# A two-layer attention and expert kernel: the zeros behind the experts' rows written a batch earlier, the gate columns folded into the linear product

## The reference, cut to what matters

```
# layer 0
o   = paged_attention(x)             # 8 heads, window 256, K/V rows through block tables
t   = o @ Wo.T
lg  = clip(t @ gate_w.T, -50, 50)    # 8 experts
top_w, top_i = top_k(lg, 2);  rw = softmax(top_w)
x   = x + t @ W.T + contrib(t, rw, top_i)     # a sparse part M[e] per expert, from 4096 masked cells
# layer 1
h   = x @ W1.T + lora(x, adapter of the batch) * scaling
p   = softmax(h @ gate1);  s, i = top_k(p, 2);  s = s / sum(s)
x   = x + sum over the two chosen experts of s * alpha * (gelu(h @ fc1[e] + b1[e]) @ fc2[e] + b2[e])
```

## Time and profile before

| | |
|---|---|
| median of 3 runs | 1142.62 us (1139.97 to 1144.23) |
| the profiled execution | 1142.49 us, span 1140.7 us |
| mean granted clock of TensorE | 0.929 of full speed |
| busy: TensorE, VectorE, ScalarE, GpSimd | 88%, 47%, 36%, 27% |
| HBM traffic over the span | 147 GB/s |
| zeros to `rows_d` | 2 x 8 DMAs of 258 KB, 3.7 us to landing |

### The profile page before, as it was taken

One profiled execution on the slowest core, in us unless ns is written; L12 is line 12 of the kernel. 1 busy time (PEld: TensorE's weight loads), 2 busy tenths in 40 slices (PEclk: granted clock), 3 DMA queues, 4 the chain that ended last, 5 costly groups with the idle time before them and its releaser, 6 DMA issues.

```text
span 1140.7 us, 18892 instructions
## 1 busy us (share of the span) xinstructions
PE 999.9 (88%) x5042; PEld 678.0 (59%) x5043; DVE 535.7 (47%) x2106; ACT 405.5 (36%) x1185; POOL 306.6 (27%) x250
## 2 busy tenths in 40 slices
PE   5999949899999899808889997999289999999994
PEld 2464447677777677604444445666167777777772
DVE  5768874455455677442334442555423333333331
ACT  3434313555565555301111111112124444444440
POOL 3000140357654141111334440233202221122221
PEclk9989956899999999958999998999689999999998
DMA  8756540354453343238787745884443333333330
GB/s 266 238 215 214 198 162 21 94 131 112 127 157 114 112 153 112 75 130 228 210 221 125 137 84 166 303 332 160 149 139 67 68 62 72 72 65 67 57 59 2
DMA packets 82417, 156.25 MB, mean 137 GB/s; under 512 B 16023, under 2 KB 28999, under 8 KB 80768
## 3 DMA queue, kind: packets, MB, share of 16 engines
q1 hardware_dynamic: 40336, 86.99, 23.2%
q0 software_dynamic: 25520, 45.11, 19.1%
q10 hardware_dynamic: 16512, 23.60, 6.5%
HBM read 94.05 MB, written 73.19 MB: 147 GB/s over the span
## 4 chain that ended last, share of the span: by engine, by line
PE 64%; DVE 14%; issue 8%; DMA 7%; DVEq 2%; ACT 2%; SPq 2%; POOL 0%; ACTq 0%; POOLq 0%
PE ps L630 44%; PE ps L711 7%; PE ps L636 4%; DMA acc<-R,tok_i 4%; PE ps L701 3%; PE ps L694 3%; DVE R L1334 1%; DVE R L1326 1%; DVE R L1344 1%; PE ps L875 1%; DMA R<-rows 1%; DVE R L1337 1%; ACT R L977 1%; SPq L392 1%; SPq L391 1%
## 5 line engine op out<-in xcount | busy, mean ns | idle before, releaser
L630 PE MATMUL ps<-R 128*128 128x128 f32 (+4 forms) x2640 | 676.4, 413 | 20.1 <-DMA R<-in_x_t 11.5
L630 PEld LDWEIGHTS ps<-R 128*128 128x128 f32 x2640 | 395.9, 194 | 259.3 <-issue 242.4
L636 PE MATMUL ps<-ident,R 128*128 128x128 f32 x504 | 77.8, 286 | 67.2 <-DMA R<-rows 54.4
L602 POOL DMA_INDIRECT out_x<-R,tok_i x39 | 60.9, 1562 | 252.2 <-DVEq L1773 165.1
L530 POOL DMA_INDIRECT rows<-R,slot_i x64 | 67.1, 1048 | 203.5 <-DVEq L1521 180.6
L636 PEld LDWEIGHTS ps<-ident,R 128*128 128x128 f32 x504 | 62.2, 152 | 94.9 <-issue 77.1
L711 PEld LDWEIGHTS ps<-R 128*128 128x128 f32 x768 | 96.4, 199 | 20.0 <-ACT R L993 16.6
L711 PE MATMUL ps<-R 128*128 128x64 f32 x768 | 99.4, 281 | 4.8 <-ACT R L993 4.8
L1410 DVE CUSTOM_DVE_ANT_0 R<-ps,R 128x384 f32<-128x384 f32 x128 | 66.0, 553 | 75.2 <-issue 75.0
L987 ACT ACTIVATE R<-R,nmx 128x384 f32<-128x384 f32 x128 | 77.5, 607 | 58.8 <-DVE nmx L1410 58.7
L602 POOL DMA_INDIRECT acc<-R,tok_i x39 | 60.6, 1553 | 128.4 <-DVE R L1675 123.3
(11 more groups left out here) (281 smaller groups left out, 924.8 us busy)
## 6 DMA issues: line engine op xcount, KB each, us to landing
R<-rows SPq DMA_DIRECT2D x78, 258.0 KB, 3.4
R<-in_fc ACTq DMA_DIRECT2D x16, 1024.0 KB, 5.6
m_buf<-R SPq DMA_DIRECT2D x8, 1024.0 KB, 5.1
R<-m_buf SPq DMA_DIRECT2D x16, 512.0 KB, 3.9
R<-acc SPq DMA_DIRECT2D x32, 256.0 KB, 5.4
rows<-zrow SPq DMA_DIRECT2D x16, 258.0 KB, 3.7
new_kv<-R SPq DMA_DIRECT2D x16, 256.0 KB, 2.1
qn<-R SPq DMA_DIRECT2D x16, 256.0 KB, 2.5
```

Source lines behind the costliest of these rows:

```text
L602: po.indirect_dma_start(out=sums[s], out_offset=bass.IndirectOffsetOnAxis(ap=tok_i[:, s:s + 1], axis=0), in_=y_sb[s], in_offset=None, boun ...
L630: m = pe.matmul(out, lhs(k), rhs(k), start=(k == 0 and first), stop=(k == KC - 1 and last))
L636: m = pe.transpose(out[:, k * P:(k + 1) * P], src[:, k * P:(k + 1) * P], ident[:])
```

## The change

Zeros: `end_i` is taken before the last batch is placed, so the zeros cover three times 128 rows from there; SyncE issues them then and waits for nothing, and GpSimd waits for them before it sends the last batch's rows. Cells: 9, 9 and 10 in GpSimd's batches 1 to 3; pieces of `m_buf` are fetched from period 3 on, and one addition step is made in each step from 8B + j = 34 on. The periods are all written out. The last tile's projection of attention goes to banks 2 and 3, upper half first, and ScalarE copies it. `choose` makes one instruction of two. Linear stage: `w1_t` and `lora_b` have 520 columns, each product is made in halves of 256 and 264, ScalarE copies both halves and the logits, and the softmax over eight is replaced by one exponential of the difference of the two chosen logits. Allocations and semaphore names are left out below.

```
@@ periods @@
-            period(0, "first", 0, 0)
-            with eng.Fori(0, 2) as i:
-                period(2 * i + 1, "mid", 1, i)
-                period(2 * i + 2, "mid", 0, i)
...
+            for B in range(NB):
+                period(B, "first" if B == 0 else "last" if B == NB - 1 else "mid", B % 2, (B - 1) // 2)
@@ SyncE @@
             for b in range(NB - 1):
+                for m in range(4 * b - 14, 4 * b - 12) if b >= 4 else ():
+                    sp.wait_ge(S["m_done"], m - 1)
+                    fetch_m(m)
                 sp.wait_ge(S["bk"], uses(b, "mid" if b else "first")["q0"] + 1)
...
-                if b == 4:
+                if b == 3:
                     sp.wait_ge(S["mscat"], 16 * ST)
                     for m in range(2):
                         fetch_m(m)
-                if b >= 5:
-                    for m in range(7 * (b - 5) + 2, min(7 * (b - 4) + 2, 16)):
-                        sp.wait_ge(S["m_done"], m - 1)
-                        fetch_m(m)
+                for m in range(4 * b - 12, 4 * b - 10) if b >= 4 else ():
+                    sp.wait_ge(S["m_done"], m - 1)
+                    fetch_m(m)
+            for m in range(14, 16):
+                sp.wait_ge(S["m_done"], m - 1)
+                fetch_m(m)
@@ zero_ends @@
-                    end = sp.value_load(end_i[0:1, e:e + 1], min_val=0, max_val=ROWS - P * NE)
-                    sp.dma_start(rows_d[bass.ds(end, P), :].rearrange("p (h n) -> p h n", h=2),
-                                 zrow[:].unsqueeze(1).broadcast_to([P, 2, DX // 2])).then_inc(S["zrows"], 16)
-                sp.wait_ge(S["zrows"], 16 * NE * n)
+                    end = sp.value_load(end_i[0:1, e:e + 1], min_val=0, max_val=NE * REGION - 3 * P)
+                    sp.dma_start(rows_d[bass.ds(end, 3 * P), :].rearrange("(p a) (h n) -> p (a h) n", a=3, h=2),
+                                 zrow[:].unsqueeze(1).broadcast_to([P, 6, DX // 2])).then_inc(S["zrows"], 16)
@@ GpSimd @@
-                t = 4 + 7 * (b - 1)
-                add = b <= 4
+                t = 4 + 9 * (b - 1)
+                add = b <= 3
...
                 if add:
-                    cells(t + 6)
+                    for u in range(t + 6, t + 9 if b < 3 else ST):
+                        cells(u)
             for b in (NB - 2, NB - 1):
                 po.wait_ge(S["r_slot"], b + 1)
+                if b == NB - 1:
+                    po.wait_ge(S["zrows"], 16 * NE)
                 for t in (2 * b, 2 * b + 1):
+                    if t == NT - 1:
+                        po.wait_ge(S["e_row"], 2)
...
                 po.wait_ge(S["r_slot"], NB + b + 1)
+                if b == NB - 1:
+                    po.wait_ge(S["zrows"], 16 * NE * 2)
@@ TensorE, behind attention and linear @@
-            project(at, "a1")
-            project(at, "h1")
+            pe.wait_ge(bc, at["o1"] + 1)
+            half("h1", 2).then_inc(S["e_in"], 1)
+            half("a1", 3).then_inc(S["e_in"], 1)
...
-                    chunks(ps[:, 4 + s, :], lambda k: x1_t[s][:, k, :], lambda k: w1_t[:, k, :], last=False)
+                    chunks(ps[:, 4 + s, 0:D // 2], lambda k: x1_t[s][:, k, :], lambda k: w1_t[:, k, 0:D // 2], last=False)
...
-                    pe.matmul(ps[:, 4 + s, :], xa_t[s], lora_b[:], start=False, stop=True).then_inc(S2["c_h"][s], 1)
-                    wait(pe, S2["c_lg"][s], i)
-                    chunks(ps[:, 6 + s, 0:NE], lambda k: x1_t[s][:, k, :], lambda k: w1_g[:, k, :], last=False)
-                    pe.matmul(ps[:, 6 + s, 0:NE], xa_t[s], b_g[:], start=False, stop=True).then_inc(S2["c_g"][s], 1)
+                    pe.matmul(ps[:, 4 + s, 0:D // 2], xa_t[s], lora_b[:, 0:D // 2], start=False, stop=True).then_inc(S2["c_h"][s], 1)
+                    chunks(ps[:, 6 + s, 0:DG - D // 2], lambda k: x1_t[s][:, k, :], lambda k: w1_t[:, k, D // 2:DG], last=False)
+                    pe.matmul(ps[:, 6 + s, 0:DG - D // 2], xa_t[s], lora_b[:, D // 2:DG], start=False, stop=True
+                              ).then_inc(S2["c_g"][s], 1)
@@ ScalarE, linear @@
-                ac.activation(x2_rows[:, 2 * i + s, 0:D], ps[:, 4 + s, :], ACT.Copy).then_inc(S2["c_x2"][s], 1)
+                ac.activation(x2_rows[:, 2 * i + s, 0:D // 2], ps[:, 4 + s, 0:D // 2], ACT.Copy)
+                ac.wait_ge(S2["c_g"][s], i + 1)
+                ac.activation(x2_rows[:, 2 * i + s, D // 2:D], ps[:, 6 + s, 0:D // 2], ACT.Copy)
+                if s == 0:
+                    ac.wait_ge(S["r_sel"], NB + i)
+                ac.activation(lg[:, s, :], ps[:, 6 + s, D // 2:DG - D // 2], ACT.Copy).then_inc(S2["c_x2"][s], 1)
@@ VectorE @@
-                    TT(t1[:], src[:], b3(best2[:, c, :]), ALU.is_equal)
-                    ve.drain()
-                    TT(t1[:], t1[:], rb(rev[:]), ALU.mult)
+                    for t in range(2):
+                        ve.scalar_tensor_tensor(t1[:, t, :], src[:, t, :], best2[:, c, t:t + 1], rev[:], ALU.is_equal, ALU.mult)
...
                     if j == 7 and last:
+                        ends()
                         row_low(at, "a2", 2 * B)
-                    if isinstance(B, int) and 8 * B + j >= 42:
-                        for _ in range(ADDS[j]):
-                            next(adds, None)
+                    if 8 * B + j >= 34:
+                        next(adds)
...
                 if not first:
-                    for _ in choose(1):
+                    routed(i - 1)
+                    for _ in place1(i - 1):
                         pass
...
+                    if not more:
+                        ends()
```

More of the change, by code:

```diff
@@ L281, in program @@
                 "last": ("a0", "h0", "o1", "a1", "h1", "o0", "rt", "a2"),
-                "after": ("h2", "o1", "a1", "h1", "rt")}
+                "after": ("h2", "o1", "rt")}
         NF, NM, NL = (len(USES[k]) for k in ("first", "mid", "last"))
@@ L719, in tail, with half @@
                 turn4(ps[:, 0, :], o_sb).then_inc(bk, 1)
+            def half(x, b):
+                lo, hi = (0, D // 2) if x[0] == "a" else (D // 2, DG)
+                return chunks(ps[:, b, 0:hi - lo], lambda k: o_t[:, k, :], lambda k: w_o[:, k, lo:hi])
             def project(at, x):
                 wait(pe, bc, at[x])
-                if x[0] == "a":
-                    chunks(ps[:, 0, 0:D // 2], lambda k: o_t[:, k, :], lambda k: w_o[:, k, 0:D // 2]).then_inc(bk, 1)
-                else:
-                    chunks(ps[:, 0, 0:DG - D // 2], lambda k: o_t[:, k, :], lambda k: w_o[:, k, D // 2:DG]).then_inc(bk, 1)
+                half(x, 0).then_inc(bk, 1)
             def cell_sums(at):
@@ L848, in _ @@
             pe.wait_ge(S["w5"], 48)
+            pe.wait_ge(S["w1_ok"], 1)
             def turn_x1(i, s):
@@ L1090, in outs @@
                         turned(i + 1, s)
+                    if s == 0 and (not isinstance(i, int) or i > 0):
+                        soft(i - 1)
                 ac.drain()
@@ L1466, in choose @@
                     ve.drain()
-                    TT(t1[:], src[:], b3(best2[:, c, :]), ALU.is_equal)
-                    ve.drain()
-                    TT(t1[:], t1[:], rb(rev[:]), ALU.mult)
+                    if c == 1:
+                        gap = TT(diff[:], best2[:, 1, :], best2[:, 0, :], ALU.subtract)
+                        if layer == 1:
+                            gap.then_inc(S["r_l"], 1)
+                    for t in range(2):
+                        ve.scalar_tensor_tensor(t1[:, t, :], src[:, t, :], best2[:, c, t:t + 1], rev[:], ALU.is_equal, ALU.mult)
                     ve.drain()
@@ L1507, in place @@
                 TT(run[:], run[:], t2[:, 0, :], ALU.add)
+                if layer == 1:
+                    TS(rs2[:], ew[:, 0, :], 1.0, None, ALU.add)
                 ve.drain()
                 TT(run[:], run[:], t2[:, 1, :], ALU.add)
+                if layer == 1:
+                    ve.reciprocal(best2[:, 0, :], rs2[:])
                 yield
+                ve.drain()
                 TT(t3, chosen_e[:], t1[:].unsqueeze(1).broadcast_to([P, 2, 2, NE]), ALU.mult)
+                if layer == 1:
+                    TT(best2[:, 1, :], best2[:, 0, :], ew[:, 0, :], ALU.mult)
                 ve.drain()
@@ L1527, in place0, with ends @@
                 return place(a_rows, t, 0, ps[:, 0, 0:2 * NE], ps[:, 0, 2 * NE:4 * NE], (bc, 1))
+            def ends():
+                ve.drain()
+                CP(end_i[:], run[:])
+                ve.drain().then_inc(S["r_end"], 1)
             def tiles():
@@ L1534, in tiles @@
                 ve.drain()
-                CP(end_i[:], run[:])
-                ve.drain().then_inc(S["r_end"], 1)
                 step(TT(ntf[0][:], run[:], region0[:], ALU.subtract))
@@ L1699, in place1, with routed @@
                 ve.memset(junk[:, 3:4], 0.0)
+                ve.wait_ge(S["r_lexp"], i + 1)
+                ve.memset(junk[:, 2:3], 0.0)
```

(32 more changed lines are left out.)

45 lines of the change are left out of this document (17 added, 28 removed).

## The result

The changed kernel took 1147.87 us (median of 20 runs, 1144.01 to 1153.65), the kernel before on the same chip 1143.08 us (median of 20, 1139.97 to 1146.10). The ratio is 1.0041, with a 95% interval of 1.0029 to 1.0053: slower, by less than the half per cent that I had set as the bound. The forecast was 1129.7 with 1112 to 1142, so the median lies above the range; the prediction gave a result within half a per cent of no change a chance of 0.12, and a gain beyond it 0.78. The profiled execution took 1146.05 us, with a span of 1143.1 us (before: a span of 1140.7).

The account below looks back on a forecast made before the run. TensorE's matrix products were taken as the bound (64% of the last-ending chain), plus a few stalls. From 1142.49 us: linear -10.0, gap 1 -11.6, gap 2 +7.8, attention +1.0, together -12.8, giving 1129.7 us; range 1112 to 1142.

Parts of the forecast that it names:

- Z: Time from the zeros' first issue to their landing, before each expert stage; forecast 24 us for 6.34 MB at 334 GB/s.
- From the landing to TensorE: First gap, from zeros landed through the last four blocks and the row fetch to TensorE's first turn: 10.6 us.
- The zeros' bound by transfer and not by issues: Both gaps: transfer outlasts seven issue distances of 1.34 us; the rival, bound by issues, said 1112.3 us, chance 0.12.
- The first sign named for being wrong: Both gaps: the forecast would be wrong if the zeros landed in under 16 or over 30 us.
- a burst three times the old one's time: Rival for both gaps: zeros take 38 us, total +15.2 us, 1157.7 us; chance 0.08.
- Gap 1: Between attention and layer 0's experts: zeros issued a batch early start TensorE at 505.9 instead of 517.48 us, -11.6.
- Gap 2: Between linear stage and layer 1's experts: the larger zeros, covered by one short round, delay TensorE by 7.8 us.
- E: End of TensorE's last gate product in the linear stage; zeros were forecast to start 0.4 us behind it.
- Attention: Period 5's stall goes (-6.8 us), but late corrections and a late addition add waits; net +1.0, ends -6.8 and +7.2.
- its two waits: Attention: TensorE waits 2 to 5 us for corrections, addition 5.8 us late; overlapping, some 7.8 us with the slow clock.
- Linear stage: Gate columns folded into wider products save 1.5 us a round, 12.0 over eight; less 2 for late sums, -10.0 us.
- The limit of 375 GB/s: Linear stage: most that DMA could move, against 391 GB/s needed in a 12.15 us round, so fc2 loads may slip.

Follow-up runs that it names:

- Kernels 1: Zero bursts alone, without the computation: 1032-byte packets as in the changed kernel moved 234 GB/s, the 6.34 MB taking 27 us; whole run 247.07 us.
- kernel 4: Changed kernel with zeros over 256 instead of 384 rows per expert (4.23 MB): 1128.98 us, ratio 0.9880 to the kernel before.
- kernel 5: Changed kernel with the same 384 rows of zeros sent in half as many packets of 2064 bytes: 1134.60 us, ratio 0.9822 to the kernel before.
- kernel 9: Bursts alone, without the computation, varying packet size and start: 337 to 343 GB/s at multiples of 1024 or 1280 bytes, 238 and 205 otherwise.
- Kernel 3: Changed kernel with GpSimd's fetches of keys and values ahead of batch 3's cells and blocks: 1150.17 us, ratio 1.0090 to the kernel before.
- Kernel 7: Changed kernel with old 128-row zeros, cells 8, 8, 8, 4, additions from turn 38, m_buf fetches moved up: 1121.83 us, ratio 0.9717 to the kernel before.
- kernel 2: Changed kernel with the zeros alone undone (128 rows per expert, after the last batch): 1124.99 us, ratio 0.9854 to the kernel before.
- kernels 6: Changed kernel with zeros and the order of cells, additions and fetches undone: 1129.74 us, ratio 0.9773 to the kernel before.
- kernel 8: Kernel 7 with zeros in whole rows, four DMAs issued by SyncE and four by ScalarE: 1113.20 us, ratio 0.9633 to the kernel before.

## Why the prediction was wrong

**The failing step is the burst's duration.** The prediction said: "In 14 us the queue moved 2.64 MB at a 56.5% share: 334 GB/s when busy", and so Z = 24 us. Measured were 32.4 and 31.7. As it counts in both gaps, it is 8.4 + 7.7 = 16.1 us, and the whole miss in spans is 2.4 + 12.8 = 15.2. Kernels 1, 4, 5 and 9 show the cause: 1032-byte packets without gaps run at about 238 GB/s once a burst lasts, and at 333 only in its first 2 us. By kernel 9 it is where they start: all fast packets of this size started on multiples of 1024 or 1280 bytes, and of those 1032 bytes apart nearly all start elsewhere. In the whole kernel only the size of the packets was changed (kernel 5), not their place. The old burst came in eight short pieces 1.34 us apart, as the rates of the kernel before from 500 to 514 us show, in slices of 0.35 us:

```profile
GB/s 0 94 211 293 246 234 340 355 221 203 339 348 121 62 357 319 21 159 354 242 0 233 354 168 0 310 348 97 50 351 330 24 139 351 266 0 0 0 0 0
```

Most pieces reach 348 to 357 and are over before a slow stretch could begin. So the rate was read rightly and applied to a stretch in which it doesn't hold. That the whole miss is so near the burst's alone is in part luck: attention came 3.8 us worse than forecast and the linear stage 4.7 us better.

**What held in that part.** From the landing to TensorE: 10.8 against 10.6. The zeros' bound by transfer and not by issues: yes (an issue every 2.5 us instead of 1.34 looks like a queue pushed back by what it carries, and with two thirds of the bytes, in kernel 4, eight issues took 13.20 us instead of 18.39). The first sign named for being wrong, a landing beyond 30 us, is what happened. The rival that came nearest was the one that I gave 0.08, a burst of three times the old one's time: it had Z = 38, too long, and not this cause, but it said that the change loses from Z = 30.4. With Z of 32 it lost.

**Gap 1: forecast -11.6, measured -2.3** in the table, of which +8.4 is Z and the rest the later start of the zeros: they went out at 476.07, 1.1 us behind the slots, instead of 0.4. **Gap 2: forecast +7.8, measured +16.2**, of which 7.7 is Z and 0.6 the start at E + 1.0.

**Attention: forecast +1.0, measured +4.8.** The mechanism was right: the stall of period 5 went, and the scatters in front of the corrections made a new one in the period before it. Of its two waits the first was the large one, 7.22 us for the corrections and 1.15 for the addition. They went out 0.9 us late by my reckoning; but behind the issue they took over 7 us to be usable, for which I had 3.3 to 6.3. One period cost 11.5 us where the forecast had 7.8. Kernel 3 shows that keys and values ahead of batch 3's cells don't lower the sum. Kernel 7, with eight cells a batch, has no wait over 1.7 us, but it changed more than that number, so what decides stays open.

**Linear stage: forecast -10.0, measured -14.7.** Right in sign, a third too small. The round is 11.70 and not 12.15 us: folding saved 1.95 us a round, because a tile's products take 4.39 us (737.16 - 732.77) or 4.47 (730.42 - 725.89, less 0.06 for the counts) and not 4.65. The limit of 375 GB/s that I read from a share of 0.93 was wrong: from 728 to 745 us the changed kernel moved 409. The 2 us that I charged for late sums were right in size, one wait of 2.27, behind which the granted clock stayed at 1.00 (741.9 to 743.0). This term isn't steady. In kernels 2 and 4 the stage took 4 to 5 us longer (795.26 - 689.40 = 105.9 and 790.87 - 684.35 = 106.5 from its first turn to its last count, against 101.7): the same wait was 2.80 and 3.27 us there, and behind it the clock was 0.61 and 0.52 for 2 us. In kernels 6 and 7 there was no such wait, and the stage took 100.2 and 100.3.

**The two figures beside the forecast.** The Trainium skill (DMA: Bandwidth & Descriptors, Bandwidth and Anatomy of one DMA) has 358 and 436 GB/s, from which I had estimated a Z of 22 and 18. For this burst both were further off than the row of the trace; the measurement decides for about 240.

## What to carry to other kernels

A bandwidth read from a short or broken burst is that of its beginning; before a burst is made three times as large, run it alone at its new length and with its own packets. Look at where each packet starts as well as at its size: here 8 bytes over 1024 in the rows' halves cost 30% of the rate. And when work is moved a batch ahead to hide it, ask how many bytes it gains on the way: zeros for three blocks instead of one, hidden behind one batch, were slower than one block in the open (kernel 2), and that was slower than one block on two queues (kernel 8).

## What the runs showed of the hardware

- Zeros from SBUF to DRAM, eight DMAs on one queue: 1024-byte packets at multiples of 1024 bytes 343 GB/s, the same 16 bytes off 205; 1032-byte packets without gaps 238, at multiples of 1280 bytes 337; 2064-byte packets 358 to 383 and 6192-byte packets 415, though without gaps they too start off such multiples: larger packets lose less.
- The DMA share hides it: it is 1.01 to 1.08 for the bursts at 337 GB/s and more, and 1.10 to 1.13 for those at 205 to 238. A share near one says that engines are occupied, not that bytes move.
- A slow burst starts at 333 GB/s for 2 us before it falls to 238.
- Idle times of TensorE in the linear stage: behind one of 2.27 us the granted clock stayed at 1.00, behind those of 2.80 and 3.27 us it was 0.61 and 0.52 for 2 us.
- How fine the grid is on which a packet has to start was not measured: the starts that gave 337 GB/s and more were multiples of 1024 and 1280 bytes, those that gave less were 16 bytes off a multiple of 1024, or 1032 bytes apart. Rows at a distance of 2304 bytes, written as whole rows, would put every packet on a multiple of 256. This was not tried in the kernel, since the indirect sends address rows without gaps, so what it would give is open.
